# Interleaved rotary queries and absorbed keys, and written-out group loops, in an attention kernel on one Trainium2 core

## The reference, cut to what matters

```python
h = x @ WA + bA
kv_lat, q_lat = jnp.split(h, 2, axis=-1)
kRt = _rope(h @ WB + bB, 0)
qRt = _rope(h @ WC + bC, 0)
...
q = (q_lat @ WUQ).reshape(b, t, NH, DH).transpose(0, 2, 1, 3)
k = (kv_lat @ WUK).reshape(b, t, NH, DH).transpose(0, 2, 1, 3)
v = (kv_lat @ WUV).reshape(b, t, NH, DH).transpose(0, 2, 1, 3)
qf = jnp.concatenate([q, qRt], axis=-1)
kf = jnp.concatenate([k, jnp.broadcast_to(kRt[:, None], (b, NH, t, DHR))], axis=-1)
scores = jnp.einsum('bhqd,bhkd->bhqk', qf, kf) * dk ** (-0.5)
attn = jax.nn.softmax(scores, axis=-1)
out = jnp.einsum('bhqk,bhkd->bhqd', attn, v)
return out.transpose(0, 2, 1, 3).reshape(b, t, NH * DH) @ WZ + bZ
```

## Time and profile before

| | |
|---|---|
| median of 3 runs | 1902.49 us (1901.72 to 1905.27) |
| the profiled execution | 1901.88 us, span 1899.7 us |
| instructions in the span | 29080 |
| PE busy | 1811.5 us (95% of the span) |
| DVE, ACT, POOL busy | 923.3, 632.1, 706.6 us |

### The profile page before, as it was taken

One profiled execution on the slowest core, in us unless ns is written; L12 is line 12 of the kernel. 1 busy time (PEld: TensorE's weight loads), 2 busy tenths in 40 slices (PEclk: granted clock), 3 DMA queues, 4 the chain that ended last, 5 costly groups with the idle time before them and its releaser, 6 DMA issues. The chain is left out here.

```text
span 1899.7 us, 29080 instructions
## 1 busy us (share of the span) xinstructions
PE 1811.5 (95%) x10664; PEld 1428.4 (75%) x10664; DVE 923.3 (49%) x1579; ACT 632.1 (33%) x1090; POOL 706.6 (37%) x524
## 2 busy tenths in 40 slices
PE   6899999999999999999999997999999999999997
PEld 4577776777777677777777776888888888888886
DVE  3565766556665665666433585233424242323332
ACT  4333333333343332333223212333333333333332
POOL 1231322213131231323100024666657575757564
PEclk9899999999999999999999998999999999999999
DMA  7000101001010100102034115124303330422011
GB/s 263 23 1 18 51 6 62 2 28 40 17 51 7 62 1 18 50 10 70 12 99 139 40 62 178 55 43 134 68 21 88 110 66 0 122 99 44 0 22 22
DMA packets 68714, 104.53 MB, mean 55 GB/s; under 512 B 12448, under 2 KB 29600, under 8 KB 68640
## 3 DMA queue, kind: packets, MB, share of 16 engines
q1 hardware_dynamic: 53568, 76.92, 12.1%
q0 software_dynamic: 7200, 16.78, 5.0%
q10 hardware_dynamic: 7872, 9.71, 1.4%
HBM read 78.23 MB, written 25.17 MB: 54 GB/s over the span
## 5 line engine op out<-in xcount | busy, mean ns | idle before, releaser
L1891 DVE CAST hh<-hid 128x512 fp32r<-128x512 f32 x128 | 95.5, 746 | 437.0 <-ACT hid L1818 437.0
L443 POOL TENSOR_TENSOR prob<-prob,rinv 128x512 f32<-128x512 f32 x64 | 66.9, 1045 | 474.5 <-DVE rinv L702 474.5
L96 PE MATMUL bank_o<-Mh,mix_h 128*128 128x512 f32 x512 | 214.4, 419 | 30.1 <-DVE x_res L709 28.7
L1734 POOL TENSOR_TENSOR w1l<-w_raw,w1h 128x512 fp32r<-128x512 f32 x112 | 185.0, 1651 | 146.3 <-ACT w1h L1810 146.2
L96 PE MATMUL e_h<-xh,w1h 128*128 (+1 forms) x512 | 200.8, 392 | 6.3 <-POOL w1l L1734 6.3
L98 PE MATMUL bank_o<-Mh,mix_l 128*128 128x512 f32 x512 | 203.8, 398 | 0.0
L97 PE MATMUL bank_o<-Ml,mix_h 128*128 128x512 f32 x512 | 203.2, 397 | 0.0
L96 PE MATMUL e_y<-w2h,hh 128*128 128x512 f32 x512 | 200.8, 392 | 1.5 <-DVE hl L1893 1.2
L97 PE MATMUL e_h<-xl,w1h 128*128 (+1 forms) x512 | 199.8, 390 | 0.0
L98 PE MATMUL e_h<-xh,w1l 128*128 (+1 forms) x512 | 199.7, 390 | 0.0
L98 PE MATMUL e_y<-w2h,hl 128*128 128x512 f32 x512 | 199.4, 389 | 0.0
(11 more groups left out here) (305 smaller groups left out, 3513.2 us busy)
## 6 DMA issues: line engine op xcount, KB each, us to landing
w_raw<-in_W_dram SPq DMA_DIRECT2D x56, 512.0 KB, 4.2
stage<-in_x_dram SPq DMA_DIRECT2D x8, 1024.0 KB, 6.0
x_res<-in_x_dram SPq DMA_DIRECT2D x32, 256.0 KB, 2.6
out_dram<-x_res SPq DMA_DIRECT2D x32, 256.0 KB, 2.0
flat_dram<-flat_sb ACTq DMA_DIRECT2D x32, 256.0 KB, 2.0
rows<-out_dram SPq DMA_DIRECT2D x4, 1024.0 KB, 5.2
stage<-in_W_dram SPq DMA_DIRECT2D x8, 512.0 KB, 5.2
x_res<-out_dram SPq DMA_DIRECT2D x3, 1024.0 KB, 5.0
```

Source lines behind the costliest of these rows:

```text
L96: nc.tensor.matmul(out, ah, bh, start=start and n == 0, stop=False)
L443: nc.gpsimd.tensor_tensor(prob[:, i % 2, :, :], prob[:, i % 2, :, :], rinv[:, :].unsqueeze(2).to_broadcast([P, HB, C]), ALU.mult).then_inc ...
L1734: nc.gpsimd.tensor_tensor(w1l[:, k, :, :], w1_at(pair, chunk), w1h[:, k, :, :].bitcast(F32), ALU.subtract).then_inc(S["w1_lo"], 1)
L1891: nc.vector.tensor_copy(hh[:, k, :], hid[:, k, :]).then_inc(S["h_hi"], 1)
```

## The change

It has two parts. (1) In the preparation of a group, the rotary products of pairs 0 to 3 go through `bank_p0` alone and the absorbed keys 0 to 3 through `bank_p1`, one of each in turn, on PE and on ACT. Absorbed keys 4 to 7 follow, and then the four heads of `wz(g, 6)` in one piece. On DVE the fourth turn of the queries now stands ahead of `x2_tile(g, 5)`. The waits follow from the new banks. (2) `over_groups` writes `body` out for all eight groups on ACT, DVE, POOL and SP.

```diff
+        def q_bank(u):
+
+            return 0 if u < UB else u % 2
+
+        def key_bank(h):
+
+            return 1 if h < UB else h % 2
...
             first()
-            with eng.Fori(0, NG - 1) as g:
-                body(g, True)
-            body(NG - 1, False)
+            for g in range(NG):
+                body(g, g < NG - 1)
...
-                nc.scalar.activation(raw[:, (u + 1) % 2, :], bank_p[u % 2][:, :], ACT.Identity, bias=K["bC"][:, u:u + 1]
+                nc.scalar.activation(raw[:, (u + 1) % 2, :], bank_p[q_bank(u)][:, :], ACT.Identity, bias=K["bC"][:, u:u + 1]
...
-                nc.scalar.copy(kabs[:, h % HB, :], bank_p[h % 2][:, :]).then_inc(S["ka_ev"], 1)
+                nc.scalar.copy(kabs[:, h % HB, :], bank_p[key_bank(h)][:, :]).then_inc(S["ka_ev"], 1)
...
                     for u in range(UB):
                         q_raw(g + 1, u)
-                    for h in range(HB):
+                        keys_absorbed(g + 1, u)
+                    for h in range(UB, HB):
                         keys_absorbed(g + 1, h)
...
                     keys_rope(g + 1)
-                    for u in range(UB - 1):
+                    for u in range(UB):
                         queries_rope(g + 1, u)
                 x2_tile(g, 5)
                 if more:
-                    queries_rope(g + 1, UB - 1)
                     less_max(g + 1, 0)
...
                 elif u:
-                    pe.wait_ge(S["raw_ev"], g * NR + u)
+                    pe.wait_ge(S["raw_ev"], g * NR + (u if u > UB else u + 1))
...
             def keys_absorbed(g, h):
-                if h % HB < 2:
-                    pe.wait_ge(S["raw_ev"], g * NR + h // HB * UB + 4 + h % HB)
+                if h == 0:
+                    pe.wait_ge(S["raw_ev"], g * NR + 1)
+                elif h < UB:
+                    pe.wait_ge(S["ka_ev"], g * NH + h)
+                elif h == UB:
+                    pe.wait_ge(S["raw_ev"], g * NR + 1 + UB)
+                elif h in (HB, HB + 1):
+                    pe.wait_ge(S["raw_ev"], g * NR + h)
                 else:
                     pe.wait_ge(S["ka_ev"], g * NH + h - 1)
...
                     for u in range(UB):
                         q_rope_mm(g + 1, u)
+                        keys_absorbed(g + 1, u)
                         wz(g, 5, (4 + u, ))
-                    keys_absorbed(g + 1, 0)
-                    keys_absorbed(g + 1, 1)
-                    for k in range(4):
-                        wz(g, 6, (k, ))
-                        keys_absorbed(g + 1, 2 + k)
-                    keys_absorbed(g + 1, 6)
-                    keys_absorbed(g + 1, 7)
+                    for h in range(UB, HB):
+                        keys_absorbed(g + 1, h)
+                    wz(g, 6, (0, 1, 2, 3))
                     prob_transpose(g, 7)
```

More of the change, by code:

```diff
@@ L549, in first @@
                     q_raw(0, u)
-                for h in range(HB):
+                    keys_absorbed(0, u)
+                for h in range(UB, HB):
                     keys_absorbed(0, h)
@@ L856, in q_rope_mm @@
                 elif u:
-                    pe.wait_ge(S["raw_ev"], g * NR + u)
+                    pe.wait_ge(S["raw_ev"], g * NR + (u if u > UB else u + 1))
                 cols = slice(u * P, (u + 1) * P)
-                split_product(nc, bank_p[u % 2][:, :], [((W["WCh"][:, i, cols], W["WCl"][:, i, cols]),
+                split_product(nc, bank_p[q_bank(u)][:, :], [((W["WCh"][:, i, cols], W["WCl"][:, i, cols]),
                                                          (lat_h[:, i, :], lat_l[:, i, :])) for i in range(2)]
@@ L868, in keys_absorbed @@
                 cols = slice(h * P, (h + 1) * P)
-                split_product(nc, bank_p[h % 2][:, :], [((W["Ah"][:, cols], W["Al"][:, cols]),
+                split_product(nc, bank_p[key_bank(h)][:, :], [((W["Ah"][:, cols], W["Al"][:, cols]),
                                                          (lat_h[:, 0, :], lat_l[:, 0, :]))]
```

## The result

| | before | changed |
|---|---|---|
| median of 4 runs each | 1903.06 us (1901.72 to 1905.27) | 1877.8 us (1875.81 to 1879.22) |
| the profiled execution | 1901.88 us | 1876.96 us |

The ratio is 0.9865, with a 95% interval of 0.9848 to 0.9882: 25.3 us less by the medians, 24.9 by the profiled executions. The forecast was 1873.6, 28.3 less; the time lies inside the range.

The account below looks back on a forecast made before the run. PE's stops for DVE's residual add at group boundaries, and the low clock behind them, bound the kernel. 7 x (4.7 - 0.7) + 0.3 = 28.3 us off 1901.9 gives 1873.6 us; range 1865 to 1887.

Parts of the forecast that it names:

- The bound: Attention stretch: PE busy 110.67 of 115 us, so gains must come from PE's stops or its clock, mean 0.96.
- PE's stop: Ahead of wz(g, 6) at each group boundary: still about 2.3 us, from 515.6 to 517.9, instead of 4.13.
- The first queries turn: On DVE at a boundary: each of the first three queries turns takes 2.78 us, 0.35 of it delay by POOL.
- a turn longer than 3 us: Sign on DVE's timeline: the forecast is wrong if the turns themselves get longer than 3 us.
- The clock: Behind PE's stop at boundaries: falls at some, not others; 0.7 us booked each, half of 1.45, bounds 0 and 2.5.
- the 28.0 us booked for the boundaries: Seven group boundaries, each 4.7 us less up to the transpose, minus 0.7 for the clock: 7 x (4.7 - 0.7).
- The groups follow each other every: Sign in the changed kernel's profile: groups should follow each other every 108.7 us or so instead of 112.7.
- The first group: Same order without wz: scores, at 82.03 before, start about 81.7; 0.3 us less, between 1 more and 1 less.
- The written-out loops: Group loops on the engines other than PE: jumps hidden, no gain taken; at most 0.6 us a boundary, 4 in all.
- The rival that gave the jumps a gain: Faster start behind the jump returns at most PE's 2.6 us wait for DVE's low mix part: 1871.0 us, chance 0.05.
- sine products with a delay by POOL: DVE's first three queries turns: POOL's cosine stretches each sine product from 0.75 to 1.10 us, 0.35 a turn.
- its worst case: Upper bound for a disturbed queries turn on DVE: as long as the keys turn, 3.69 us, its final add 1.66.

Follow-up runs that it names:

- e2: The kernel before, in its old order, with the four group loops written out: 1884.8 us, ratio 0.9911.
- e5: The kernel before, loops kept, with DVE's residual add of tile 5 moved between the second and third queries turns: 1867.38 us, ratio 0.9821.
- e10: The kernel before with DVE's group loop alone written out: 1902.11 us, ratio 1.0.
- e9: The kernel before with POOL's group loop alone written out: 1900.94 us, ratio 0.9997.
- e1: The changed kernel with the four group loops jumping as before, so the new order alone: 1880.79 us, ratio 0.9882.
- e3: The changed kernel with DVE's residual add of tile 5 put back between the third and fourth queries turns: 1852.35 us, ratio 0.9739.
- e4: The changed kernel with POOL's cosines of pairs 0 to 3 cut to one of 8 batches in groups 1 to 7: 1855.88 us, ratio 0.9749.

## Why the prediction was right, and where it was not

**The bound** was read rightly: PE's stop for the residual add and the low clock behind it were all there was to gain, and the gain stands in the attention stage, 24.4 of 24.9 us.

**PE's stop** came out at 2.27 us where 2.3 was forecast, with the restart 17.56 us behind `rope_keys` instead of 17.3. The first queries turn is longer than booked, 3.04 us instead of 2.78, for its sine product takes 1.38 us and not 1.10; the next two are shorter, 2.72, and the last is 2.17 instead of 2.13. So one of the forecast's own signs of being wrong, a turn longer than 3 us, did come up, by 0.04 us. The sine product goes on for 0.55 us behind POOL's cosine in that turn too (496.12 + 1.30 to 496.58 + 1.38); the mechanism was right, but that cosine has a lead of 0.46 us over the sine product, where the keys' cosine had 0.74, and so holds it longer:

```profile
496.12 1.30 POOL L443 TENSOR_TENSOR q_rope<-rope_raw,table_attend 128x512 f32<-128x512 f32 x1 [1.02 <-ACT rope_raw L525]
```

**The clock** is the term that was mis-sized. The forecast said that it would fall at some boundaries, at half of 1.45 us on the mean, 0.7. It fell at five of seven and cost about 1.6 each: 5 x 1.6 / 7 = 1.14 us a boundary, 0.44 more than booked, 3.1 us over the seven. Where the clock stayed up the transpose comes 20.4 us behind `rope_keys`, 0.15 later than booked, which is 1.0 over the seven. Together these are the 28.0 us booked for the boundaries less the 23.9 measured. Outside them the profiled execution gained 1.0 us where 0.3 was booked; half of that is PE's wait for the low part of the mix (2.6 us to 2.1), the rest has no place of its own in this account. The groups follow each other every 109.6 us where the clock fell and every 108.0 where it stayed up; 108.7 were forecast.

**The first group** was to gain 0.3 us. Its scores start at 82.27 instead of 82.03 and wait for DVE's turn, as forecast. But its first matmul of `rope_keys` also starts later, at 64.59 instead of 63.99, so from there to the scores it took 17.7 us instead of 18.0. This agrees with the forecast and doesn't prove it: other traces of the old order (e2, e5 to e10) took 17.0 to 17.2 us for the same stretch, so one trace can't tell 0.3 us.

```profile
64.59 0.80 PE L96 MATMUL bank_p<-lat_h,WBh 128*128 128x512 f32 x1 [2.23 <-DVE lat_l L648]
...
82.27 1.08 PE L899 MATMUL bank_s<-k_absorbed,q 128*64 128x256 f32 x8 [1.78 <-DVE q_rope L676]
```

**"The written-out loops" is the step that failed**: "The register instructions stand ahead of waits; the pause between two turns [...] is all that they could fill." That held for DVE and POOL, whose loops cost nothing that the times can tell (e9, e10), but the step looked for the cost as idle time of the engine that jumps. What acts is no delay of that engine: the looping ACT starts its last copy 0.05 us sooner, and the price appears on DVE, as a longer instruction, 1.1 us at each of seven boundaries, and the clock besides. Alone the loops were worth 17.7 us. In the sum the error is hidden, since the new order removes the same stop: over e1 they give some 3 us, of which about 1 us (0.14 at each boundary) can be followed in the gap. That the zero did the forecast so little harm is luck, for the forecast did not know of the meeting that the new order takes away. The rival that gave the jumps a gain had 1871.0 and a different mechanism, a faster start of DVE behind the jump. Its wait, that for the low part of the mix, did get shorter, 2.1 us in 8 waits instead of 2.6, in each kernel with DVE's loop written out and in no other. This is e10, its table of PE's waits and then, on DVE's timeline, the instruction of the earlier trace rows:

```profile
PE bank_m L921 <- DVE mix_l L677: 2.1, 8, 0.3
```

```profile
428.69 0.69 DVE L689 SCALAR_TENSOR_TENSOR score<-bank_s,table_attend 128x512 f32<-128x512 f32 x1 [1.42 <-PE bank_s L896]
```

It starts after 1.42 us of idling instead of 1.51, so the jump or the register instructions beside it were not wholly hidden, as the forecast read that row; which of the two costs the 0.09 us was not tried. What that rival had right is 0.5 us in all, too little for the times to tell. The rule of the Trainium skill's page "Runtime: NRT & Kernel Launch", section on the mechanics of instruction fetch, is not what gave ACT's 13.6 us either: DVE and POOL jump as well, and gain nothing that the times can tell.

**The rows were there.** The forecast charged sine products with a delay by POOL, and took the keys turn's 1.66 us add as its worst case, but it did not ask why the turn from 509.15 to 512.70 lasts 3.55 us and not 2.43. That is the meeting with POOL that e2 shows, and without it PE's stop before the change would have been 1.1 us shorter.

**What it did not ask:** where else the add could stand. It counted what the add stands behind, and took the new place as given; e3 and e5 show that the place was worth as much as the change.

Open: in the changed kernel the first queries turn is the longest, and e4 shows that this comes from POOL's cosines. The timeline points to that of pair 1, the only one that runs beside the long product, but it was not shortened alone. Why the last boundary has a pause of 0.3 us instead of the long product was not tried. Nor is it known what in ACT's loop moves its copy.

## What to carry to other kernels

When an engine waits, list what stands ahead of the instruction that it waits for, on that instruction's engine, and ask first whether it may stand earlier: one line moved (e5) did more than the rebuilt order. Look for the same instruction with two durations in one timeline: an instruction that lasts 1.82 us here and 0.69 there is held by a neighbour, and a shift of some hundredths of a microsecond on a third engine can decide which of the two pays. Two edits that shorten the same stop don't add up, so try each alone before either is given the credit.

## What the runs showed of the hardware

**DVE and POOL hold each other out for a whole instruction.** A product or add of DVE with two SBUF inputs lasts 0.69 us alone. Where POOL's cosine has begun first, it ends some 0.55 us behind POOL: 1.82 us in the rows of before, 1.03 and 1.38 in those of the changed kernel. Where DVE is first, POOL's 1.29 us become 1.80. DVE's shuffle, with one input, lasts 0.71 to 0.77 us, with POOL beside it or not, and the residual add, with one input in PSUM, 0.68 or 0.69, beside POOL's cosine (at 219.98 us in the kernel before) as without it. The Trainium skill's page "SBUF — State Buffer", in its section on SBUF's two separate sides, describes such a lock of a shared port pair, taken by whichever starts first and against which the other blocks fully. The rows agree, but for an overlap of about 0.15 us at the end; what they add is that 0.03 us decided over 1.1.

**The granted clock behind stops of equal length differs.** With a gap of 2.50 to 3.42 us it was down at four or five of seven boundaries, within one run and at the same place in the program; with 2.05 or less at none, with 4.37 at all. In which state of the chip it falls, no run here tells.

**Written-out code is not always the quicker one to start.** Without its loop ACT began one copy 0.14 us sooner (1.35 us of idling instead of 1.49) and another 0.05 us later (0.08 us behind the shuffle that released it instead of 0.03). It was the later start that made the kernel faster.
